# Two graph layers on one core: fourteen units' codes transposed by DMA instead of TensorE, with a new order at the front and at the end

## The reference

```python
x = layernorm(x + layer0(x, adj, Wq, Wk, Wv))     # softmax over (adj + eye), times V
h = x @ W.T + b_W
e = (h @ a1)[:, None] + (h @ a2)[None, :] + b_a
e = where(e > 0, e, 0.2 * e)                      # leaky relu
scores = where(adj > 0, e, -9e15)
x = layernorm(x + softmax(scores, axis=1) @ h)
```

## Time and profile before

| | |
|---|---|
| median of 3 runs | 253.71 us (253.17 to 254.16) |
| the profiled execution | 255.0 us, of which the span of its instructions is 253.2 us |
| mean granted TensorE clock | 0.983 |
| TensorE busy (PE) | 236.2 us, 93% of the span |
| VectorE (DVE), ScalarE (ACT), GpSimd (POOL) | 185.3, 154.4, 61.4 us |
| DMA | 71.76 MB, 283 GB/s over the span |

### The profile page before, as it was taken

One profiled execution on the slowest core, in us unless ns is written; L12 is line 12 of the kernel. 1 busy time (PEld: TensorE's weight loads), 2 busy tenths in 40 slices (PEclk: granted clock), 3 DMA queues, 4 the chain that ended last, 5 costly groups with the idle time before them and its releaser, 6 DMA issues.

```text
span 253.2 us, 4017 instructions
## 1 busy us (share of the span) xinstructions
PE 236.2 (93%) x1523; PEld 133.3 (53%) x1523; DVE 185.3 (73%) x284; ACT 154.4 (61%) x182; POOL 61.4 (24%) x104
## 2 busy tenths in 40 slices
PE   5959999499999999999999999999999999999980
PEld 4947675245555555555555555555555555555450
DVE  1378787967777777779768776977777778797433
ACT  2468978989067999170489994610899982220032
POOL 3284688999200000003030000002300000032122
PEclk9999999679999999999999999999999999999998
DMA  6999999999999999999589999998499920010102
GB/s 187 365 386 389 383 387 383 387 387 386 385 388 383 380 384 387 387 386 385 64 237 305 332 403 392 387 387 298 114 299 339 397 99 3 1 41 3 41 3 88
DMA packets 40939, 71.76 MB, mean 283 GB/s; under 512 B 5843, under 2 KB 6100, under 8 KB 40916
## 3 DMA queue, kind: packets, MB, share of 16 engines
q1 hardware_dynamic: 40480, 71.33, 79.2%
q10 hardware_dynamic: 436, 0.13, 0.2%
HBM read 69.36 MB, written 2.10 MB: 282 GB/s over the span
## 4 chain that ended last, share of the span: by engine, by line
PE 86%; POOL 3%; ACT 3%; DMA 2%; DVE 2%; issue 2%; ACTq 1%; POOLq 0%; DVEq 0%
PE banks L1202 67%; PE banks L1158 10%; PE banks L1217 3%; PE banks L1095 3%; DMA brow<-in_L_gnn_b_W_dram 2%; ACT a L737 2%; PE banks L1110 1%; POOL rstd L597 1%; PE banks L1081 1%; DVE y L1036 0%; POOL f_parts L636 0%; POOL xhat_st L602 0%; POOL frstd L646 0%; POOL feat L629 0%; DVE e_sb L938 0%
## 5 line engine op out<-in xcount | busy, mean ns | idle before, releaser
L1202 PE MATMUL banks<-e_sb,f_parts 128*128 128x512 f16 x768 | 186.1, 391 | 1.5 <-DVE e_sb L938 1.1
L926 DVE SCALAR_TENSOR_TENSOR e_sb<-R,cr_word,banks 128x1024 f32<-128x1024 f32 x124 | 153.8, 1275 | 30.9 <-PE banks L1158 28.3
L737 ACT ACTIVATE a<-a_sb,code_bias 128x2048 fp8e4<-128x2048 int32 x64 | 124.3, 1997 | 2.8 <-DMA a_sb<-in_adj_dram 2.1
L1202 PEld LDWEIGHTS banks<-e_sb,f_parts 128*128 128x128 f16 x768 | 71.6, 97 | 86.8 <-issue 4.0
L646 POOL TENSOR_TENSOR frstd<-frv,minus_half 128x4 f32<-128x4 f32 x8 | 8.1, 1012 | 168.9 <-DVE frv L962 167.6
L1158 PE MATMUL banks<-ident,a 128*128 128x128 f16 x496 | 38.0, 220 | 3.6 <-ACT a L737 3.6
L1158 PEld LDWEIGHTS banks<-ident,a 128*128 128x128 f16 x496 | 32.8, 98 | 15.4 <-ACT a L737 3.9
L728 ACT COPY R<-banks 128x512 f32<-128x512 f32 x8 | 4.7, 587 | 35.9 <-PE banks L1110 35.9
L753 ACT ACTIVATE junk<-y 128x128 f32<-128x128 f32 x28 | 8.3, 298 | 26.8 <-DVE y L953 26.8
L944 DVE RECIPROCAL rden<-banks 128x4 f32<-128x4 f32 x7 | 1.3, 183 | 12.2 <-PE banks L1217 12.2
L1095 PEld LDWEIGHTS banks<-m0c_um,x_tr 128*128 128x128 f32 x64 | 9.6, 224 | 0.8
(11 more groups left out here) (113 smaller groups left out, 101.9 us busy)
## 6 DMA issues: line engine op xcount, KB each, us to landing
a_sb<-in_adj_dram SPq DMA_DIRECT2D x64, 1024.0 KB, 12.4
x_sb<-in_x_dram SPq DMA_DIRECT2D x8, 256.0 KB, 9.9
out_dram<-out_sb SPq DMA_DIRECT2D x8, 256.0 KB, 5.8
w_nat<-in_L_gnn_W_dram ACTq DMA_DIRECT2D x1, 64.0 KB, 3.2
wv<-in_L_gnn_Wv_dram ACTq DMA_DIRECT2D x1, 64.0 KB, 3.1
acol<-in_L_gnn_a_vec_dram SPq DMA_DIRECT2D x1, 1.0 KB, 3.0
bcol<-in_L_gnn_b_W_dram ACTq DMA_DIRECT2D x1, 0.5 KB, 4.5
ba<-in_L_gnn_b_a_dram ACTq DMA_DIRECT2D x1, 0.0 KB
```

Source lines behind the costliest of these rows:

```text
L737: nc.scalar.activation(a8[:, n % 2, Q * h:Q * (h + 1), k * PW:(k + 1) * PW], a_parts[:, m % SLOTS, :, :], ACT.Relu, bias=code_bias[:, :], ...
L926: nc.vector.scalar_tensor_tensor(out=e_sb[:, k % NE, :], in0=R[:, g % 2, :], scalar=cr_word[:, 0, 2 * t + b:2 * t + b + 1], in1=ps_code[s ...
L1202: ins = nc.tensor.matmul(ps_acc[g % 2][h][:, :], f[:, j, :], e_half[:, k % NE, cols, part], start=(j == 0 and n == 0), stop=(j == T - 1 an ...
```

## The change

The rows of x, `adj` and the output are dealt out anew: row 512 i + 256 e + 2p + b lies in partition p of quad i as tile 2e + b. Columns keep the same numbering, so a unit's words are now 128 neighbours in a code row, and `a8` is laid out so that the words of one unit are 1024 neighbours in a partition. A load becomes two DMAs of 512 KB, and the pieces of x and of the output go from 2 KB to 1 KB.

The last 14 units, 50 to 63, are not turned on TensorE. SyncE issues a transposing DMA for each (`move`), from `a8` to one of four buffers in SBUF that held x's turned quads; it waits for the unit's codes and, from the fifth on, for the products of four units back. VectorE's products and ScalarE's reuse of `a8` wait for its landing. Moves 50 to 55 stand in the load queue behind loads 59, 61 and 63, moves 56 to 63 behind the last load and ahead of the last stores.

In the loop FIRST = 4 becomes LATE = 9. In the front, load 0 goes ahead of x's second quad, `layer0(0)` ahead of its turning and without four warm-up matmuls, VectorE makes the first words and half products before and around quad 1's statistics and scaling, and copies the first half of R itself, and quad 1's `root` comes behind the first features. At the end column half 1 goes in two quarters: the last quarter of the last three units is summed in a bank of its own, which VectorE adds to the copied half.

```diff
-    FIRST = QUADS - 4
+    LATE = QUADS + 1
+    NM = 4
+    MOVED = 14
-    adj_t = adj.rearrange("(i p q) n -> p i q n", p=P, q=Q)
+    adj_t = adj.rearrange("(i e p b) n -> p i e b n", p=P, e=2, b=2)
...
+        at_moved = [x_tr[:, i, :].bitcast(F16).rearrange("p (r n) -> p r n", r=TG) for i in range(NM)]
+        code_moved = [x_tr[:, i, :].bitcast(F8).rearrange("p (n b) -> p n b", b=2) for i in range(NM)]
...
-                    sp.dma_start(a_parts[:, m % SLOTS, :, :],
-                                 adj_t[:, 2 * g + h, :, col:col + PW]).then_inc(a_loaded[m % SLOTS], 16)
+                    for e in range(2):
+                        sp.dma_start(a_pairs[:, m % SLOTS, e, :, :],
+                                     adj_t[:, 2 * g + h, e, :, col:col + PW]).then_inc(a_loaded[m % SLOTS], 16)
...
+                def move(s):
+                    n, c = divmod(s, 4)
+                    d = moved(s)
+                    sp.wait_ge(codes_ready, PARTS * n + 2 * (c // 2) + 2)
+                    if d >= NM:
+                        sp.wait_ge(p_ready, 2 * (s - NM + 1))
+                    else:
+                        sp.wait_ge(y0_ready, QUADS)
+                    sp.dma_start_transpose(out=at_moved[d % NM], in_=a16[:, n % 2, c // 2, c % 2, :]).then_inc(
+                        at_landed[d % NM], 16)
...
+                load(0)
                 load_x(1)
-                load(0)
...
                 for m in range(SLOTS, LOADS):
                     load(m)
+                    if m % 2 == 1:
+                        for u in (m - SLOTS - 1, m - SLOTS):
+                            if by_dma(u):
+                                move(u)
...
+                for u in range(S - SLOTS, S):
+                    move(u)
...
                     if n >= 2:
-                        act.wait_ge(at_ready, 4 * (n - 2) + 2 * (k + 1))
+                        pair = 4 * (n - 2) + 2 * k
+                        act.wait_ge(at_ready, turned(pair + 2))
+                        for u in (pair, pair + 1):
+                            if by_dma(u):
+                                moved_to(act, u)
...
                 copy_xt(0)
-                copy_xt(1)
                 act.wait_ge(consts_ready, 12)
                 codes(0)
+                copy_xt(1)
                 exps(0)
+                codes(1)
+                copy_xt(2)
                 exps(1)
-                rows(0, 0, ps_row)
-                copy_xt(2)
-                codes(1)
                 rows(0, 1, ps_row2)
...
                     if b == 0:
-                        dve.wait_ge(at_ready, s + 1)
+                        if by_dma(s):
+                            moved_to(dve, s)
+                        else:
+                            dve.wait_ge(at_ready, s + 1)
...
                 stats(0)
-                stats(1)
                 dve.wait_ge(rstd_ready, 1)
                 divide(0, scores)
                 divide(0, inner)
+                words(0)
+                stats(1)
+                dve.wait_ge(row_ready, 1)
+                nc.vector.tensor_copy(R[:, 0, 0:HW], ps_row[:, :]).then_inc(r_ready, 1)
+                half_edges(0, 0, 0)
+                half_edges(0, 1, 0)
                 dve.wait_ge(rstd_ready, 2)
                 divide(1, scores)
-                words(0)
+                half_edges(1, 0, 0)
                 words(1)
-                half_edges(0, 0, 0)
-                half_edges(0, 1, 0)
+                half_edges(1, 1, 0)
                 divide(1, inner)
-                half_edges(1, 0, 0)
-                half_edges(1, 1, 0)
...
+                    if k == 0:
+                        dve.wait_ge(half_done, 3)
+                        dve.wait_ge(acc_copied, 2 * G)
+                        nc.vector.tensor_tensor(acc_t[:, LAST:GW], ps_last[:, :], acc_t[:, LAST:GW],
+                                                ALU.add).then_inc(acc_copied, 1)
...
                 def turn(s):
+                    if by_dma(s):
+                        return
...
                 x_turned(0)
                 weights(0)
+                weights(1)
+                layer0(0)
                 x_turned(1)
-                weights(1)
-                keep_busy(bank[0], 4)
-                layer0(0)
-                layer0(1)
                 half_turn(0, 0)
                 half_turn(1, 0)
+                layer0(1)
...
-                    if FIRST < slot < S - NA:
+                    if LATE < slot < S - NA:
                         turn(slot + NA)
...
-                    if slot <= FIRST:
+                    if slot <= LATE:
                         turn(slot + 2)
-                    if slot == FIRST:
+                    if slot == LATE:
                         turn(slot + 3)
...
+                    for k in range(2):
+                        for s in units:
+                            if s == S - 1:
+                                if k == 0:
+                                    pe.wait_ge(acc_copied, 2 * G - 1)
+                                    pe.wait_ge(y_ready, 2 * G - 2)
+                                    projections(0, quad(0), range(Q)).then_inc(fin_mm, 1)
+                                else:
+                                    pe.wait_ge(acc_copied, 2 * G)
+                                    projections(1, quad(4), range(2)).then_inc(fin_mm, 1)
+                            for b in range(2):
+                                ins = products(s, b, (slice(HW, LAST), slice(LAST, GW))[k])
+                        ins.then_inc(half_done, 1)
+                    pe.wait_ge(acc_copied, 2 * G + 1)
+                    projections(1, quad(4), range(2, 4)).then_inc(fin_mm, 1)
```

More of the change, by code:

```diff
@@ L107, in graph_layers @@
         ps_row2 = bank[6]
-        ps_exp = [bank[4 + i][:, 256:256 + 2 * Q].rearrange("p (k q) -> p k q", k=2) for i in range(2)]
+        ps_exp = [bank[i][:, c:c + 2 * Q].rearrange("p (k q) -> p k q", k=2) for i, c in ((4, 256), (2, 160))]
+        ps_last = ps_row[:, 0:2 * P]
         ps_u = bank[5]
@@ L220, in graph_layers @@
         at_ready = sem("at_ready")
+        at_landed = [sem(f"at_landed{i}") for i in range(NM)]
         p_half = sem("p_half")
@@ L244, in wait_xhat, with by_dma, turned, moved @@
                 eng.wait_ge(xhat_later, i - 1)
+        def by_dma(s):
+            return s >= S - MOVED
+        def turned(s):
+            return min(s, S - MOVED)
+        def moved(s):
+            return s - (S - MOVED)
+        def moved_to(eng, s):
+            d = moved(s)
+            eng.wait_ge(at_landed[d % NM], 16 * (d // NM + 1))
         def group_at(slot, offset):
@@ L658, in _ @@
                 root(0)
+                features(0, 0)
                 root(1)
-                features(0, 0)
                 features(0, 1)
@@ L792, in _ @@
                 nc.scalar.copy(acc_t[:, 0:HW], ps_acc[g % 2][0][:, :]).then_inc(acc_copied, 1)
+                act.wait_ge(half_done, 2)
+                nc.scalar.copy(acc_t[:, HW:GW], ps_acc[g % 2][1][:, :]).then_inc(acc_copied, 1)
                 squares(g, 0)
-                act.wait_ge(half_done, 2)
-                for k in range(2):
-                    cols = slice(k * HW // 2, (k + 1) * HW // 2)
-                    nc.scalar.copy(acc_t[:, HW:GW][:, cols], ps_acc[g % 2][1][:, cols]).then_inc(acc_copied, 1)
                 act.wait_ge(frv_ready, 2 * g)
@@ L1193, in sums, with products @@
                         pe.wait_ge(p_ready, 2 * s + b + 1)
-                        products(s, b, 0)
-                        products(s, b, 1).then_inc(mm_done, 1)
-                def products(s, b, h):
+                        products(s, b, halves[0])
+                        products(s, b, halves[1]).then_inc(mm_done, 1)
+                def products(s, b, cols):
                     g, t = divmod(s, U)
                     k, j = 2 * s + b, 2 * t + b
-                    cols = slice(h * HW, (h + 1) * HW)
+                    h, first = divmod(cols.start, HW)
+                    dst, opened = ps_acc[g % 2][h][:, first:first + cols.stop - cols.start], j == 0
+                    if cols.start == LAST:
+                        dst, opened = ps_last[:, :], k == 2 * (S - HALVED)
                     for n, (f, part) in enumerate(((fl, 1), (fh, 1), (fh, 0))):
-                        ins = nc.tensor.matmul(ps_acc[g % 2][h][:, :], f[:, j, :], e_half[:, k % NE, cols, part],
-                                               start=(j == 0 and n == 0), stop=(j == T - 1 and n == 2))
+                        ins = nc.tensor.matmul(dst, f[:, j, :], e_half[:, k % NE, cols, part],
+                                               start=(opened and n == 0), stop=(j == T - 1 and n == 2))
                     return ins
```

52 lines of the change are left out of this document (27 added, 25 removed).

## The result

The kernel after takes 250.69 us (median of 4 runs, 249.71 to 250.71) against 253.60 (253.17 to 254.16) of the kernel before beside it: ratio 0.987, 95% interval 0.984 to 0.991. Its profiled execution takes 250.7 us with a span of 248.9. The forecast was 241.3, with a range of 239.5 to 250.0: the sign was right, the size was not.

A forecast was written before the change was run, and what follows sets the result against it. TensorE was taken to bound the kernel. LATE -6.3, front +0.1, fourteen units -6.3, store +0.2 and quarters -0.1 sum to -12.4 us, taking the median from 253.71 to 241.3 us, range 239.5 to 250.

The forecast's parts named there:

- The bound, and LATE = 9: TensorE bounds the kernel; summing before turning in slots 5 to 8 removes its hole at 42 to 48 us: -6.3 us.
- The order of the front: Before the sums: fewer warm-up matmuls and earlier first words, against statistics and R's copy on VectorE: +0.1 us, -0.6 to +1.3.
- Fourteen units turned by transfers: Slots 47 to 60: fourteen units' turning matmuls leave TensorE, their transfers hidden under the sums: -6.3 us.
- VectorE's products from SBUF at 1.24 us: Late slots: a product reading its codes from SBUF still costs VectorE 1.24 us, two 2.47.
- VectorE's ability to feed 2.71 us a unit: Late slots: VectorE, with the closing group's work too, keeps up with sums at 2.71 us a slot, so TensorE stays the bound.
- A transfer at 2.9 us, from the diagonal's pieces: Late units: 1024 pieces of 256 bytes at the diagonal transfer's pace take 2.9 us, under the 3.1 us allowed.
- Six slots of 2.71 us lie between such an issue and TensorE's need: From move(54) on, waiting for products four units back still leaves six slots of 2.71 us before TensorE needs the unit.
- Loads 60 to 63 wait for codes 52 to 55 anyway: SyncE's queue: these loads lose nothing by standing behind a waiting move, as they wait for those codes in any case.
- The store: End: the last store, in 1 KB pieces, takes at most 0.7 us longer than its 2.8: +0.2 us.
- the quarters: End: column half 1 in quarters, one pair of projections ahead of the last sums: -0.1 us, bounds -0.6 to +0.5.
- the first: One gain lost: hole recurs elsewhere, or (second form) VectorE's product or transfers keep late slots near 3.16 us: 247.5 us; chance 0.22.
- The slower rival: Load queue, units 50 to 63: all transfers run in series at 5.8 us each, 278.6 us by the median; chance 0.13.

The follow-up runs named there:

- experiment 1: Kernel after with none of the units moved, all 64 turned on TensorE: 250.48 us, ratio 0.985 to the kernel before.
- experiment 4: Kernel before with only the later lookahead (FIRST = 9 for 4): 248.39 us, ratio 0.977.
- experiment 2: Kernel after with eight units moved (56 to 63, behind the last load) instead of 14: 246.67 us, ratio 0.970 to the kernel before.
- experiment 8: Kernel after with eight units moved and 10 more warm-up matmuls in the front's gap on TensorE: 246.06 us, ratio 0.968 to the kernel before.
- experiment 10: Kernel after with ten units moved, 10 more warm-up matmuls in the front, and the old end: 245.61 us, ratio 0.967 to the kernel before.
- experiment 12: Kernel after with ten units moved and the front and end of the kernel before: 244.40 us, ratio 0.962 to the kernel before.
- experiment 3: Kernel after with the 14 transfers left out, their buffers holding a constant (output wrong): 243.82 us, ratio 0.959 to the kernel before.
- experiment 9: Kernel after, all fourteen moved, without loads 56 to 63 (output wrong): 243.93 us, ratio 0.960 to the kernel before.
- experiment 11: Kernel after with ten units moved and 10 more warm-up matmuls in the front, end in quarters: 245.06 us, ratio 0.965 to the kernel before.
- experiment 5: Kernel after with the transfers of units 50 to 55 issued from ScalarE's queue instead of SyncE's: 252.81 us, ratio 0.996 to the kernel before.
- experiment 7: Kernel after with ten units moved (54 to 63) instead of 14: 245.69 us, ratio 0.965 to the kernel before.

## Why the prediction failed, by its own steps

The step that failed is that of the fourteen units: it hid each transfer, at 2.9 us, under the sums, and gave it no share of the DMA engines beside the loads and no time in SyncE's queue. Beside the loads the transfers took 4.8 to 8.0 us, and the stretch that was to lose 5.8 us became 0.6 longer. The sign came from LATE (experiments 1 and 4).

- **The bound, and LATE = 9: right.** -6.3 was said, -6.2 came in the changed kernel and -6.1 alone (experiment 4). None of the next-late rows reached TensorE; the only wait on features is of 0.5 us, as before.
- **"The order of the front" (+0.1, bounds -0.6 to +1.3): mis-sized, +1.4 in the profiles.** The warm-up matmuls were priced as four instructions to be saved. What the new order did was put `half_turn(0, 0)` where TensorE waits for codes 0 and for ScalarE's copy behind them (0.8 us). In this profile 8 matmuls of `layer0(1)` behind that idle stretch take 1.84 us and 4 turns 0.85, against 0.89 and 0.45 later in the same chain: the pace of the 1.2 GHz level against 2.4, although the granted clock reads 1.00 in the window of 12 to 14 (in experiment 2 the slow stretch lies at 17.4 to 22 us). The first half product came at 18.20, not 0.4 ahead of 17.08. That this pace is what costs the front is argued from traces (experiment 8) and not shown by a time, and the new front is 1.2 us slower than the old one even when filled (experiments 10 and 12). What the rest of it is stays open.
- **"Fourteen units turned by transfers" (-6.3): this step failed, and cost the forecast.** Its parts:
  - VectorE's products from SBUF at 1.24 us: right (2.47 a pair still, 4.87 for four), and so was VectorE's ability to feed 2.71 us a unit (experiment 3).
  - A transfer at 2.9 us, from the diagonal's pieces: near it for one that has the DMA engines to itself (3.0 to 4.4, median 3.2, experiment 9), false for the first six. These flew beside loads that already filled the engines; one of each pair stands in the chain, with 5.3, 6.4 and 7.4 us. The prediction gave the transfer a duration, and no share of a resource that the loads hold at 1.05, and at 1.01 in the stretch where the transfers came (184 to 204 us of the kernel before). Of the two pages of the Trainium skill that it named, neither is what the trace shows: by "VectorE: DVE Perf Modes", the three transpose paths, a unit would be an estimated 10.5 us, where it lands in 3.2 alone; by "Advanced Engine Details and Errata", X-Bar Transpose (TRN2), an estimated 0.7, where the engines are held an estimated 1.4.
  - "Six slots of 2.71 us lie between such an issue and TensorE's need": wrong. That counts from the ring of products, but the issue also has to come up in SyncE's queue. `move(54)` had its codes near 189.1 and its place from 190.6 (half of the 4.87 us from 188.17), and was issued at 199.91. The first pair was issued at 182.81, not at 179.9, and VectorE had nothing else from 185.06 (182.59 + 2.47): the room was 2.2 us. Of the 2.9 us by which that issue came late, 1.4 are the front's and 1.2 the two issues of the halved load ahead of it.
  - "Loads 60 to 63 wait for codes 52 to 55 anyway": true of the semaphores, but it hid the loop. The issue of a transfer was given no time. Beside loads a pair's issue held SyncE's queue for 4.2 to 6.9 us, so that the loads behind it went out late (codes 54 and 55 ended by 189.1, loads 62 and 63 were issued from 197.28) and flew beside the next pair.
  - The price: VectorE idles 12.6 us. It makes a unit in 2.47 against TensorE's 2.71, wins back 0.24 a unit, and the closing group takes that. So from 207.37 its work and not TensorE's sets the end: 27.1 us to 234.4 and 6.4 more to the end of the last sum at 240.85.
- **The store (+0.2) and the quarters (-0.1): small, as said.** The last store is issued 3.1 us before the end of the span (245.78 of 248.9), where it was 2.8 (250.41 of 253.2). That the median store lands in 2.6 us where it took 5.8 isn't the pieces' doing: in experiment 1, with the same pieces, it takes 5.7. Behind the last sum 8.05 us against 8.22, with 0.45 for the projections ahead of it; the quarters alone are not settled (experiments 10 and 11).

Of the rivals, the first came, in its second form: the late slots were no faster on the whole, because transfers set their pace. Its 247.5, the front's 1.3 us and the 1.3 us that the prediction took off for the profile of the kernel before make 250.1, near the 250.69 measured. The slower rival had the right duration beside loads (5.8 us) but was applied to all fourteen, when six meet loads. Of the prediction's signs of being wrong one came, at another place: VectorE idled on DMA ahead of units 50 to 55, not behind 54 to 63. What should have been asked of the earlier trace rows is who gives way when the DMA engines are already full.

## What to carry to other kernels

Before work is moved from an engine to DMA, read the DMA share of the stretch in which it will run: at 1.0 there is nothing to take it, and it is paid for twice, by the late transfer and by the loads behind it; where the loads have ended, the same transfer cost no time here (experiment 2). Judge this by the share and not by GB/s, which fell here while the engines stayed full. And look at what stands behind the issue in its own queue: here an issue that was held for 2 to 4 us kept back the next loads, and these then flew beside the next transfers.

## What the runs showed of the hardware

- A transposing transfer of 256 KB from SBUF to SBUF takes at least 1.23 us of its queue to issue and lands in 3.0 to 4.4 us by itself (median 3.2); beside loads the issue of two takes 4.2 to 9.6 us (the kernel after, experiments 5 and 7) and the landing of one 4.8 to 11.0, from either queue. Fourteen in a row kept up with 2.7 us a unit (experiment 9). The page counts 14,784 more packets under 512 bytes than that of experiment 1, which has the same loads and no transfer: 1,056 a transfer, near the 1024 pieces of 256 bytes that the prediction supposed. Whether these short packets are why the engines move less isn't tested.
- It takes an estimated 1.4 us of all 16 DMA engines (experiment 9), about twice as much as the same bytes of load.
- In the front of the kernel after, TensorE at the pace of 1.2 GHz isn't seen in the granted clock (1.00), only in the durations; in that of experiment 2 (0.51 from 18 to 20 us) and after the hole at 204 to 208 us (0.57) it is seen.
